# Last attentions in phases: keys and values of four batches in 256-column products, transposes two scores behind

## Reference, cut to what matters

```python
h = _layer_norm(x, ln1_scale, ln1_offset)
x = x + _cross_attention(h, xf_1, wq1, bq1, wk1, bk1, wv1, bv1, wo1, bo1, bias_k1, bias_v1)
h = _layer_norm(x, ln2_scale, ln2_offset)
x = x + _cross_attention(h, xf_2, wq2, bq2, wk2, bk2, wv2, bv2, wo2, bo2, bias_k2, bias_v2)
h = _layer_norm(x, ln_mlp_scale, ln_mlp_offset)
x = x + gelu(h @ w_fc1 + b_fc1) @ w_fc2 + b_fc2
# _cross_attention: one more key and value (bias_k, bias_v) for every batch
logits = einsum('bqhk,bthk->bhqt', q_in @ wq + bq, concat(kv_in @ wk + bk, bias_k)) / sqrt(K)
ctx = einsum('bhqt,bthk->bqhk', softmax(logits), concat(kv_in @ wv + bv, bias_v))
out = ctx @ wo + bo
```

## Time and profile before

| | before |
|---|---|
| median of 3 runs | 1144.05 us (1143.9 to 1145.86) |
| the profiled execution's own time | 1143.24 us |
| its span, first to last instruction | 1141.2 us |
| mean granted clock of PE | 0.979 of full speed |
| busy: PE | 1052.6 us, 92% |
| busy: DVE, ACT, POOL | 55%, 43%, 36% |

### The profile page before, as it was taken

The page is one execution under the profiler, slowest core; times in us unless marked ns, Lnnn a source line. Parts: engine busy times, 40 slices in busy tenths (PEclk is TensorE's granted clock), DMA queues, the critical chain, the costliest instruction groups (busy, mean ns, idle before and its releaser), DMA issues.

```text
span 1141.2 us, 17011 instructions
## 1 busy us (share of the span) xinstructions
PE 1052.6 (92%) x6772; PEld 811.6 (71%) x6772; DVE 626.6 (55%) x1070; ACT 487.2 (43%) x973; POOL 415.1 (36%) x438
## 2 busy tenths in 40 slices
PE   6999889887899799998999999999999999978998
PEld 3666555444567588878777777777777777657997
DVE  3656788677566522751454445675444544564552
ACT  2556676665666322224333223333233333324543
POOL 2534689799866411320221122231122211222230
PEclk9999999998999899999999999999999999999999
DMA  9000000000000350000000013310000000100000
GB/s 309 30 2 1 1 1 1 1 2 1 1 2 1 121 193 1 1 0 1 1 1 1 1 37 111 111 38 1 1 1 1 1 1 6 69 1 1 29 20 29
DMA packets 17043, 32.22 MB, mean 28 GB/s; under 512 B 3522, under 2 KB 8388, under 8 KB 16452
## 3 DMA queue, kind: packets, MB, share of 16 engines
q1 hardware_dynamic: 16964, 31.13, 7.9%
HBM read 29.03 MB, written 2.10 MB: 27 GB/s over the span
## 4 chain that ended last, share of the span: by engine, by line
PE 72%; POOL 10%; ACT 8%; issue 6%; DVE 3%; DMA 0%; POOLq 0%; DVEq 0%
PE work L715 10%; PE work L827 10%; PE scores L766 9%; PE work L783 5%; PE scores L679 5%; PE work L692 5%; PE work L816 4%; POOL pair L1698 3%; PE work L411 2%; PE work L533 2%; PE scores L524 2%; PE work L577 2%; PE work L798 2%; POOL pair L1701 2%; PE work L490 2%
## 5 line engine op out<-in xcount | busy, mean ns | idle before, releaser
L827 PE MATMUL work<-pair,probsT 128*128 128x256 f32 x512 | 122.0, 392 | 11.0 <-ACT pair L1577 8.8
L1657 POOL TENSOR_SCALAR stat<-stat 128x2 f32<-128x2 f32 (+1 forms) x49 | 11.1, 227 | 316.8 <-DVE stat L936 315.4
L715 PE MATMUL work<-ctxT,w 128*128 128x128 f32 x1024 | 120.2, 275 | 3.5 <-ACT pair L1568 1.6
L827 PEld LDWEIGHTS work<-pair,probsT 128*128 128x128 f32 x512 | 96.9, 194 | 35.9 <-issue 20.3
L715 PEld LDWEIGHTS work<-ctxT,w 128*128 128x128 f32 x1024 | 118.2, 192 | 5.2 <-issue 3.1
L766 PE MATMUL scores<-pair,act_bufs 128*128 128x512 f32 x256 | 115.2, 592 | 0.0
L1568 ACT ACTIVATE pair<-work 128x512 f32<-128x512 f32 x64 | 38.2, 598 | 154.3 <-PE work L783 154.3
L1558 ACT ACTIVATE kvT<-work,cols 128x128 f32<-128x128 f32 x128 | 36.6, 369 | 154.5 <-PE work L715 154.5
L1802 POOL TENSOR_TENSOR probs<-probs,smax 128x1024 f32<-128x1024 f32 x22 | 42.0, 1907 | 159.3 <-DVE smax L1253 159.3
L1233 DVE TENSOR_REDUCE smax<-scores 128x16 f32<-128x1024 f32 x32 | 39.2, 1225 | 77.1 <-PE scores L766 77.1
L766 PEld LDWEIGHTS scores<-pair,act_bufs 128*128 128x128 f32 x256 | 46.4, 190 | 46.0 <-issue 45.9
(11 more groups left out here) (165 smaller groups left out, 2375.6 us busy)
## 6 DMA issues: line engine op xcount, KB each, us to landing
w<-in_l_wk SPq DMA_DIRECT2D x8, 512.0 KB, 6.2
w<-in_l_wq SPq DMA_DIRECT2D x8, 512.0 KB, 6.8
w<-in_l_wv SPq DMA_DIRECT2D x8, 512.0 KB, 7.2
w<-in_l_wo SPq DMA_DIRECT2D x8, 512.0 KB, 8.0
out<-x SPq DMA_DIRECT2D x8, 256.0 KB, 2.2
x<-in_x SPq DMA_DIRECT2D x1, 1536.0 KB, 9.5
pair<-in_l_fc SPq DMA_DIRECT2D x1, 1024.0 KB, 7.2
pair<-in_l_pr SPq DMA_DIRECT2D x1, 1024.0 KB, 9.3
```

The costliest lines, as they stand in the source:

```text
L715: last = mm(bank[:, h * P:(h + 1) * P], w[:, c, (4 * g + h) * K3:(4 * g + h + 1) * K3], ctxT[:, c, p * P:(p + 1) * P], start=(c == 0), sto ...
L827: last = mm(step_banks(j + 1)[0][:, 0:D], probsT_bufs[j % 2][:, q, :], pv[n % 2][:, bb, q, :], start=(q == 0), stop=(q == GH // 2 - 1))
```

## The change

Keys and values are now made for **four batches** at a time (256 context columns): 16 units m = 4n + g, for the four quads n (two of each attention). A projection is 8 matmuls of 256 columns, key products 8 of 256 columns, value products 16 as wide as before. The products of a whole quad are held in one buffer `kv_products`, and quad n is worked off in two phases: first its four units (no tile between them), then its 8 tiles. Key products go through `sc`, and the projections and value products through `work`. In the tile phase the scores of tile j + 2 stand ahead of the transposes of tile j, whose output product follows directly. The residual of tile j - 1 must be done before the output product of tile j, as both use `work[2]`. `mlp_source(0)` moves ahead of the last tile's transposes. The second attention's weights are asked for in the unit phase of quad 1.

```diff
-            for j in STEPS:
-                key, value, i = key_of(j), value_of(j), input_of(j)
-                if key is not None:
-                    key_projection(j, key)
-                if value is not None:
-                    value_projection(j, value)
-                if tile_of(j) is not None:
-                    tile_scores(j)
-                if key is not None:
-                    key_products(j, key)
-                if tile_of(j - 1) is not None:
-                    tile_transposed(j - 1)
-                if value is not None:
-                    value_products(j, value)
-                if tile_of(j - 1) is not None:
-                    tile_output(j - 1)
...
+            def tile_output(j):
                 e.wait_ge(a_lpT, 2 * j + 2)
+                e.wait_ge(d_lr, j)
                 for q in range(GH // 2):
+                    last = mm(work[2][:, 0:D], probsT_bufs[j % 2][:, q, :], pv[:, j // 2 % 4, q, :],
                               start=(q == 0), stop=(q == GH // 2 - 1))
...
+            for n in range(QUADS):
+                for g in range(4):
+                    m = 4 * n + g
+                    key_projection(m)
+                    if n == 0 and g < 2:
+                        tile_source(g)
+                    if n in (0, 2) and g == 2:
+                        value_constants(attention_of(n))
+                    value_projection(m)
+                    key_products(m)
+                    value_products(m, 0)
+
+                    if g == 3:
+                        tile_scores(TILES * n)
+                    value_products(m, 1)
+                    if g == 3:
+                        tile_scores(TILES * n + 1)
+                for i in range(TILES):
+                    j = TILES * n + i
+                    if i + 2 < TILES:
+                        tile_scores(j + 2)
+                    tile_transposed(j)
+                    tile_output(j)
+                    s = 4 * n + 2 + i // 2
+                    if i % 2 == 0 and s < 2 * B:
+                        tile_source(s)
+                    if j == 4 * B - 2:
+                        mlp_source(0, True)
```

DVE's list is written anew in the same way:

```diff
+                tile_shifted(TILES * n)
+                tile_shifted(TILES * n + 1)
+                tile_sums(TILES * n)
+                for i in range(TILES):
+                    j, s = TILES * n + i, 4 * n + 3 + i // 2
+                    if i > 0:
+                        tile_residual(j - 1)
+                    if i % 2 == 1 and s - 1 < 2 * B:
+                        tile_source(s - 1)
+                    if i + 1 < TILES:
+                        tile_sums(j + 1)
+                    if i + 2 < TILES:
+                        tile_shifted(j + 2)
...
+                    if n == 3 and i >= 4:
+                        for q in range(2):
+                            weight_low((i - 4) // 2, 2 * (i % 2) + q)
+                    if n == 3 and i in (4, 5):
+                        last_norm(i - 4)
+                if n == 3:
+                    last_source(0)
+                tile_residual(TILES * n + 7)
```

More of the change, by code:

```diff
@@ L115, in build @@
         PAIR = 2 * (DC * GS + GH // 2 * D + GS)
[L116 to L119, removed]
+        pairs = sb("pairs", [P, 2 * PAIR])
+        pair = [pairs[:, i * PAIR:(i + 1) * PAIR] for i in range(2)]
+        pair_at = [nc.sbuf_base - 4 * (2 - i) * PAIR for i in range(2)]
         x = sb("x", [P, B * TT, D])
@@ L136, in build @@
         stat = [sb(f"stat{i}", [P, 48]) for i in range(4)]
-        kvT = [sb(f"kvT{i}", [P, 4, P]) for i in range(3)]
+        keysT = sb("keysT", [P, 4, 4 * S])
         act_bufs = sb("act_bufs", [P, 4, DC * T])
@@ L707, in tensor @@
                         hidden(b, f)
[L710 to L739, removed]
@@ new lines, in key_projection @@
+            def key_projection(m):
+                n, g = divmod(m, 4)
+                e.wait_ge(s_in[f"l3_wk{attention_of(n)}_{g}"], 16)
+                for half in range(2):
+                    if m == 0:
+                        e.wait_ge(d_mr, B)
+                    elif g == 0:
+                        e.wait_ge(a_lpT, 2 * TILES * n)
+                    else:
+                        e.wait_ge(a_pv, 4 * (m - 1) + half + 1)
+                    for h in range(2):
+                        k = 4 * g + 2 * half + h
+                        for c in range(DC):
+                            last = mm(bank_c[half][:, h * D:(h + 1) * D], w3_wk[:, c, k * K3:(k + 1) * K3],
+                                      ctxT[:, c, n % 2 * D:(n % 2 + 1) * D], start=(c == 0), stop=(c == DC - 1))
+                    last.then_inc(pe_kp, 1)
@@ L1580, in tile_exponentials, with value_products @@
+            def value_products(m, q):
+                n, g = divmod(m, 4)
+                e.wait_ge(pe_f2, B)
+                e.wait_ge(pe_lo, TILES * n)
+                for half in range(2):
+                    e.wait_ge(pe_pv, 4 * m + 2 * q + half + 1)
+                    act(pv[:, 2 * half:2 * half + 2, 2 * g + q, :],
+                        work[2 * q + half][:, :].rearrange("p (b d) -> p b d", b=2), ACT.Copy).then_inc(a_pv, 1)
             def tile_exponentials(j):
```

480 lines of the change are left out of this document (236 added, 244 removed).

## The result

The changed kernel takes 1164.36 us in the median of 4 runs (1160.91 to 1165.75), against 1143.97 us of the kernel before, run beside it. The ratio is 1.0174, with a 95% interval of 1.0144 to 1.0204: 20.4 us slower, where +17 was forecast. The profiled execution took 1165.75 us with a span of 1164.0 us and a mean granted clock of 0.972.

A forecast was written before the change was run, and what follows sets the result against it. PE's own instructions were taken to set the time. On the part's 526.2 us, -5.3, -31.3, +25.6, +20.8 and +7.1 gave 543.1, which is +16.9, so 1161 us, range 1147 to 1172.

The forecast's parts named there:

- Step 1: Projections and key products in unit phases: half as many, wider records save 5.3 us; value products 0.
- weight loads pace narrow products: Rival for projections and key products: wide records as short as narrow ones, -85.7 us, 1075 at the far end; chance 0.01.
- Step 2: Whole changed part: all idle time and slow clock of the kernel before go, -31.3 us.
- Step 3: Between each tile's transposes and output product: ACT's copies lie bare, 0.80 us for 32 tiles, +25.6 us.
- Step 4: Four tile-phase starts: PE waits 3.3 us for first probabilities, then slow clock; 5.2 each, +20.8 us.
- clock term: At each of four tile-phase starts: slow clock after PE's 3.3 us idle costs 1.9 us.
- Step 5: Inside tile and unit phases, and at tile phases' ends: no new PE waits, 0 us.
- Step 6: End of the last tile phase: output 30 waits 4.3 us for DVE, clock 2.0, 0.8 after last output; +7.1 us.
- the starts are covered: Rival at four starts and the end: no PE wait left, 1133 us; chance 0.05 faster, 0.05 the same.
- short gaps cost clock: Rival in tile phases: 0.8 us idles lower the clock to 0.95 or DVE falls behind, 14 more, 1175; chance 0.05.

The follow-up runs named there:

- e4b: Changed kernel with each 256-column projection and key-product matmul made as two of 128 columns, one half finished before the other; 1168.00 us.
- e1: Changed kernel with each tile's output product, and DVE's residuals, moved one tile later; 1136.72 us, ratio 0.9938 to the kernel before.
- e2: Changed kernel with DVE's sums of the first tile ahead of the second tile's shift at each tile phase's start; 1144.90 us.
- e6: e2 with ACT's copies of the first tile's transposes ahead of the second tile's exponential; 1140.16 us.
- e3: Changed kernel with two weight splits and the second MLP-source norm behind tile 29's residual, later ones behind the last residual; 1161.89 us.
- e8: Changed kernel with e1, e2 and e3 edits, but second norm ahead of the last residual, last four splits behind the MLP's second source; 1113.02 us.

## Why the prediction was right, step by step

**Direction and size.** The forecast was 1161 us and the median 1164.36. The sum held because its large terms were read from rows that showed the very situation in the kernel before. The medians look closer than the forecast was: for the profiled execution the sum said 1160.1 and 1165.75 was measured, 5.6 us apart. The forecast added 0.8 us from profile to median, and here the median stands 1.4 below the profile, which is luck. The steps' own misses all go the same way, so between steps none cancel.

**Step 1** was right in size and in its reason that a record's time goes with its columns, but not in where all of it comes from. The units gave 4.8 us instead of 5.3. Of the 0.30 us of a unit only 0.14 are the three wide sets (3.56 + 3.45 + 3.55 = 10.56, before 2 x 3.57 + 2 x 1.78 = 10.70). The other 0.16 are the value products, 3.60 against 2 x 1.88, which the step had put at 0. Compared in the same order of work, against e4b, the three sets are worth 0.36 a unit, 5.8 us in all. The rival that weight loads pace narrow products is refuted, since e4b's records take 3.57 / 32 = 112 ns. The Trainium skill ("TensorE: Matmul & The Clock Gate", section "Back-to-back issue gap") gives some 81 ns for each matmul of 128 columns in such a stream. A record of two would take 162 ns, an estimate from that figure; the measurement decides.

**Step 2** was right: no wait of the earlier trace rows is left at its place.

**Step 3** was right: 1.77 from transposes to output product in the one place of the earlier trace rows became 31 such places. e1 shows that it is the distance in PE's list that costs. It also shows a price that my sum did not see: separated, the pair takes another 0.2 us less than in the changed kernel.

**Step 4** had the mechanism, DVE's second shift ahead of the first sums, with a wait of 3.03 for 3.3. Its clock term was mostly too small: 3.2, 2.0, 3.1 and 1.8 us against 1.9. e2 and e6 confirm it, 22.8 us together. The step looked at one list, though. ACT had the same fault behind DVE's, hidden by the wait for POOL, and it took over 2.31 us at the first start and 1.33 at the others as soon as that wait was gone.

**Step 5** was right inside the phases. Its sentence that unit phases have no wait left out `value_constants`: two waits of 0.6 for a late row, +1.3 us with what follows. Of the 4.9 us between 543.1 and 548.0 step 4 makes 1.5, these waits 1.3, the scores A 0.8, step 1 0.5, step 6 0.4 and the first set 0.35.

**Step 6** was right: output 30 was late by 4.33 us (forecast 4.3), the clock took 2.55 (2.0), 0.64 stood behind the last output (0.8). e3 confirms DVE's order as the cause, and shows that the work set aside is not free: 3.8 of its 6.4 us come back in the MLP until norm and splits have a better place (e8).

**The other rivals.** That the starts are covered is refuted by the four waits. That short gaps cost clock is refuted too: between the starts the tiles have their 0.74 us idle and output products of 3.72, and the window over the rest of the first tile phase has full clock (length, PE busy, clock, DMA):

```profile
596.00:648.00 52.00, 46.84 (x210) 1.00 0.00 0
```

**What the change is worth.** The loss is in the order of the lists. With output products one tile later, DVE's first sums ahead, and the last norm and splits placed anew, the same phases and widths run 2.6% faster than the kernel before (e8), or 2.4% without the difference ahead of the part. ACT's order of e6 was not tried in e8, where a tile's copies have another tile's scores beside them.

## What to carry to other kernels

When interleaved work is pulled apart into phases, look at each consumer that now stands directly behind its producer: a copy of 0.8 us that other work had hidden is paid once per tile. Then walk every in-order list across each phase's first and last tiles, where the distance is shortest, and mend the lists together, since the next one's fault is hidden behind the first. Side work put behind a critical residual must still be early enough for the next stage.

## What was unexpected of the hardware

**The port that DVE shares with POOL.** DVE's timeline in the changed kernel at the first start, then POOL's:

```profile
581.85 0.17 DVE L1233 TENSOR_TENSOR smax<-smax,probs 128x16 f32<-128x16 f32 x1
...
583.42 0.90 DVE L1233 TENSOR_TENSOR smax<-smax,probs 128x16 f32<-128x16 f32 x1
```

```profile
582.39 1.90 POOL L1798 TENSOR_TENSOR probs<-probs,smax 128x1024 f32<-128x1024 f32 x1 [30.42 <-DVE smax L1235]
```

An addition of 16 columns takes 0.17 us, but 0.90 when it falls beside POOL's multiplication, and it ends where POOL's ends (583.42 + 0.90 = 584.32, against 582.39 + 1.90 = 584.29). The Trainium skill ("SBUF — State Buffer", section "Who interferes with whom") says that a DVE instruction with two SBUF inputs contends with a GpSimd instruction that reads SBUF, and that the port pair they share is an exclusive lock; these rows agree. The next tile's clamp, 16 columns with one input (L1217), fared alike: at 585.72 it took 0.90 in place of 0.17 and ended with POOL's next multiplication (586.62, against 584.69 + 1.90 = 586.59). A tiny operation can so bring 0.7 us of waiting into a tile's way.

**The clock after a wait.** The same 3.03 us of idle PE was followed by 3.2, 2.0, 3.1 and 1.8 us of loss at half clock in four starts. Among shorter waits, 1.33 us (e2) and 2.02 (e3) were followed by output products of 3.72, but 2.31 (e2) by one of 5.41 and 2.28 by one of 5.38. The length of a wait alone does not give its price here, and what sets it was not isolated.
